# A post-norm decoder kernel: the end of its cross attention in one stage, top-k selection and first attention reordered

## The reference, cut to what matters

```
# block 2: cross attention
sim = einsum('bihd,bjhd->bhij', x @ Wq, ctx @ Wk) * SCALE
out = einsum('bhij,bjhd->bihd', softmax(sim), ctx @ Wv) @ Wo + bo
# block 5: 4 heads, 256 keys, the 32 greatest scores kept
scores = where(mask, Q K / sqrt(32), -inf)
topv, topi = top_k(scores, 32);  attn = scatter(softmax(topv), topi)
c_t = (mean of attn over the heads) @ V
x  = layernorm(x_text) * (1 + gate*scale_in) + gate*shift_in    # scale, shift = split(c_t @ W_film_in + b)
y  = s4d(x) * (1 + gate*scale_out) + gate*shift_out             # the same with W_film_out
xt = x_text + y
xt = xt + gelu(layernorm(xt) @ W1 + b1) @ W2 + b2
out5 = layernorm(xt) * g_norm_out + b_norm_out
x  = layernorm(x_text + out5)                                   # then block 6
```

## Time and profile before

| | |
|---|---|
| Median of 3 runs | 2426.15 us (2425.98 to 2428.31) |
| Profiled execution's own time | 2428.74 us |
| Its span, mean granted TensorE clock | 2426.9 us, 0.947 |
| PE busy | 2136.3 us (88%) |
| DVE busy | 1609.0 us (66%) |
| ACT busy | 999.0 us (41%) |
| POOL busy | 884.2 us (36%) |

### The profile page before, as it was taken

How to read it: one execution, slowest core, us unless ns; L and a number is a source line. 1 busy time by engine, 2 the same in 40 slices (tenths; PEclk the granted TensorE clock), 3 DMA queues, 4 the chain that set the end, 5 groups by cost and what they waited for, 6 DMA issues and landing times. The chain is left out here.

```text
span 2426.9 us, 33828 instructions
## 1 busy us (share of the span) xinstructions
PE 2136.3 (88%) x12230; PEld 1469.4 (61%) x12230; DVE 1609.0 (66%) x4155; ACT 999.0 (41%) x2097; POOL 884.2 (36%) x510
## 2 busy tenths in 40 slices
PE   8688888998997899499896888999698899999997
PEld 3255555642664789266474444447555788888886
DVE  6799999722657212456326999512489888888886
ACT  2498988511765331435424776141101321221210
POOL 0298888201541895324102655512301211101110
PEclk9799999999998999699998888999899999999998
DMA  3121111000005567300101000110210000000001
GB/s 100 47 81 48 49 48 49 9 11 0 1 1 177 193 204 240 113 1 2 59 1 42 1 1 1 42 78 1 89 51 3 1 1 1 1 1 1 1 1 36
DMA packets 63274, 108.56 MB, mean 45 GB/s; under 512 B 12482, under 2 KB 44098, under 8 KB 61444
## 3 DMA queue, kind: packets, MB, share of 16 engines
q1 hardware_dynamic: 61572, 102.20, 12.6%
q0 software_dynamic: 1536, 4.20, 0.5%
HBM read 93.40 MB, written 12.98 MB: 44 GB/s over the span
## 5 line engine op out<-in xcount | busy, mean ns | idle before, releaser
L766 POOL TENSOR_TENSOR XT<-mamba_DU,scan_BS 128x1024 f32<-128x1024 f32 x128 | 299.0, 2364 | 144.9 <-DMA scan_BS<-mamba_rows 107.5
L895 DVE TENSOR_TENSOR_SCAN scan_H<-scan_AB,XT 128x512 f32<-128x512 f32 x256 | 296.2, 1208 | 7.9 <-POOL XT L766 4.9
L3129 PE MATMUL ex_HP<-XT,pe_DOWN 128*128 128x256 f32 x1024 | 250.2, 391 | 6.0 <-PEq L2865 5.2
L3190 ACT ACTIVATE ex_GH<-ex_HP 128x512 f32<-128x512 f32 x128 | 76.4, 598 | 381.0 <-PE ex_HP L3129 346.2
L3160 PE MATMUL ex_OP<-pe_UP,ex_GH 128*128 128x256 f32 x1024 | 231.5, 380 | 0.0
L780 PEld LDWEIGHTS scan_TP<-ident,scan_H 128*128 128x128 f32 x1024 | 120.2, 142 | 156.9 <-DVE scan_H L895 81.1
L825 ACT ACTIVATE scan_AB<-mamba_E,mamba_AA 128x510 f32<-128x510 f32 x256 | 198.6, 776 | 37.6 <-DVE scan_H L895 33.2
L3129 PEld LDWEIGHTS ex_HP<-XT,pe_DOWN 128*128 128x128 f32 x1024 | 194.6, 195 | 31.6 <-issue 5.3
L3160 PEld LDWEIGHTS ex_OP<-pe_UP,ex_GH 128*128 128x128 f32 x1024 | 194.5, 191 | 25.8
L789 PE MATMUL scan_YT<-mamba_BC,ident 128*128 128x512 f32 x384 | 198.4, 599 | 4.1 <-ACT scan_YS L841 2.3
L780 PE MATMUL scan_TP<-ident,scan_H 128*128 128x128 f32 x1024 | 147.7, 278 | 45.6 <-DVE scan_H L895 45.5
(11 more groups left out here) (449 smaller groups left out, 4434.0 us busy)
## 6 DMA issues: line engine op xcount, KB each, us to landing
moe_W<-in_L_ffn_w SPq DMA_DIRECT2D x32, 1024.0 KB, 7.6
scan_BS<-mamba_rows SPq DMA_DIRECT2D x64, 256.0 KB, 3.2
pe_DOWN<-in_L_ffn_down SPq DMA_DIRECT2D x1, 4096.0 KB, 13.2
pe_UP<-in_L_ffn_up SPq DMA_DIRECT2D x1, 4096.0 KB, 22.5
moe_dispatch<-moe_BOTH SPq DMA_DIRECT2D x1, 2560.0 KB, 14.6
experts_XE<-moe_dispatch SPq DMA_DIRECT2D x16, 160.0 KB, 2.4
moe_answers<-experts_YE SPq DMA_DIRECT2D x16, 160.0 KB, 3.3
XT<-in_xT SPq DMA_DIRECT2D x4, 512.0 KB, 5.7
```

Of the source, the lines that this page charges most:

```text
L766: pool.tensor_tensor(BU[:, r % 2, cs], tokens(DU, cs, r // DS), row, ALU.mult).then_inc(bu_ready, 1)
L895: v.tensor_tensor_scan(H[:, r % 2, c], AB[:, n % 2, :], BU[:, r % 2, c], 0.0, ALU.mult, ALU.add).then_inc(h_ready, 1)
L3129: ins = pe.matmul(HP[:, n % 2, a, :], DOWN[:, k, 2 * q + a, :], XT[:, k, b * BLK:(b + 1) * BLK], start=(k == 0), stop=(k == KD - 1))
```

## The change

First attention: the one addition of BO to X is gone; after each of the 32 products POOL adds one half of BO (128 columns) to one half of a tile of X. Top-k: NM is made by ACT, at the head of `exp_all`, and DVE's L2458 is gone; ACT and DVE wait on the last strike of round 0. ACT's sums stand ahead of the copy of the pooled context, and the out half of film is a step of its own, between them. On PE the out half of unit n-2 is made between turn and pooled context of unit n-1, the in half at the end as before. At the start scores 0 come after the first queries, scores 1 after the third, and the square root, reciprocal and offset of the input norm are taken later on ACT and DVE. The end of block 5: `finish_norm` and `norm_gram` are replaced by one stage `finish_gram`, tile by tile, with 2 PSUM banks for residuals and 2 for transposes.

```diff
+                HALVES = NU // NT
                 out_loads.wait(pool)
-                add_row(pool, X, BO)
                 for m in range(NU):
                     pool.wait_ge(sum_ready, m + 1)
                     if m >= 2:
                         pool.wait_ge(turned, 2 * (m - 1))
                     pool.tensor_tensor(PN[:, m % 2], PR[:, m % 2], SM[:, m, :].rearrange("p (j o) -> p j o", o=1).to_broadcast([P, 4, S]),
                                        ALU.mult).then_inc(probs_ready, 1)
+                    part = slice(m % HALVES * (D // HALVES), (m % HALVES + 1) * (D // HALVES))
+                    pool.tensor_tensor(X[:, m // HALVES, part], X[:, m // HALVES, part], BO[:, part], ALU.add)
...
-            finish_norm(nc, "s4ln3", X, None, ident, mlp_product(HT, W2), total=lambda t: Z[:, t, :],
-                        base=lambda t: Z[:, t, :], out=lambda t: Z[:, t, :], affine=GB, needs=[mlp_loads])
-        norm_gram(nc, "s4norm", X, Z, XT, ident, FO, next_inputs.GS)
+            finish_gram(nc, "s4end", X, Z, XT, ident, FO, next_inputs.GS, mlp_product(HT, W2), GB, mlp_loads)
...
-                def film(n):
-                    for i in range(2):
-                        if n:
-                            pe.wait_ge(film_out_read if i else film_in_read, n)
+                    else:
+                        pe.wait_ge(film_out_read if i else film_in_read, n)
...
+                        pe.matmul(FP[:, i, :], CTT[:, k, n * P:(n + 1) * P], WI[:, i, k, :], start=(k == 0), stop=False)
+                    add_bias(pe, ident, FP[:, i, :], BI[:, i, :]).then_inc(film_ready, 1)
                 inputs.loads.wait(pe)
                 queries(0)
+                scores(0)
                 queries(1)
-                scores(0)
                 queries(2)
+                scores(1)
                 queries(3)
-                scores(1)
                 film_loads.wait(pe)
                 for n in range(NT + 1):
                     if n + 2 < NT:
                         scores(n + 2)
+                    if n == NT:
+                        film(n - 2, 1)
                     if n:
                         turn(n - 1)
+                    if 2 <= n < NT:
+                        film(n - 2, 1)
+                    if n:
                         pool_context(n - 1)
-                        film(n - 1)
+                        film(n - 1, 0)
+                film(NT - 1, 1)
...
                 def exp_all(n):
-                    act.wait_ge(max_ready, n + 1)
+                    act.wait_ge(first_struck, n + 1)
+                    act.activation(NM[:, n % 2, :], MX[:, n % 2, :, 0], ACT.Copy, scale=-1.0).then_inc(shift_ready, 1)
+                    act.wait_ge(shift_ready, n + 1)
...
+                def film_out(n):
                     act.wait_ge(film_ready, 2 * n + 2)
                     act.activation(FO[:, n, :], FP[:, 1, :], ACT.Copy, scale=GATE[:]).then_inc(film_out_read, 1)
...
                 queries(0)
+                scale(0)
                 queries(1)
-                scale(0)
-                queries(2)
-                queries(3)
                 act.wait_ge(stats_ready, 1)
                 act.activation(RS[:], MV[:, :, 1], ACT.Sqrt, bias=ident[:, EPS5:EPS5 + 1]).then_inc(std_ready, 1)
+                queries(2)
                 scale(1)
+                queries(3)
                 film_loads.wait(act)
...
                     if n + 2 < NT:
                         scale(n + 2)
+                    if n < NT:
+                        sums(n)
+                    if n >= 2:
+                        film_out(n - 2)
                     if 1 <= n <= NT:
                         pooled_out(n - 1)
-                    if n < NT:
...
+                def norm_scale():
                     v.wait_ge(stats_ready, 1)
...
-                            if r:
+                            if r == 1 and i:
+                                v.wait_ge(first_struck, n + 1)
+                            elif r:
                                 ch.need(struck[i])
...
+                        if r == 1 and n == 0:
+                            norm_scale()
...
                             if r == LAST and i:
                                 ins.then_inc(struck_ready, 1)
+                            elif r == 0 and i:
+                                ins.then_inc(first_struck, 1)
                             else:
                                 struck[i] = ch.mark(ins)
-                        if r == 0:
-                            v.tensor_scalar(NM[:, n % 2, :], mx[:, :, 0], -1.0, None, ALU.mult).then_inc(max_ready, 1)
...
-def norm_gram(nc, name, X, base, XT, ident, XC, GS):
...
+def finish_gram(nc, name, X, Z, XT, ident, XC, GS, residual, affine, needs):
+    LATE = 4
...
             @block.tensor
             def _(pe):
                 def turn(t):
+                    pe.wait_ge(normed2, t + 1)
+                    if t >= 2:
+                        pe.wait_ge(turned_read, t - 1)
                     for k in range(KD):
+                        ins = pe.transpose(TP[:, t % 2, k * P:(k + 1) * P], X[:, t, k * P:(k + 1) * P], ident[:, 0:P])
                     ins.then_inc(turned, 1)
                     if t == 0:
                         pe.matmul(RP[:, 0:D], ident[:, ONES:ONES + P], X[:, 0, :], start=True, stop=True)
                         for k in range(KD):
                             ins = pe.matmul(RC[:, k:k + 1], X[:, 0, k * P:(k + 1) * P], ident[:, ONES:ONES + 1], start=True, stop=True)
                         ins.then_inc(row_ready, 1)
+                def gram(t):
+                    if t == 0:
+                        pe.wait_ge(ones_ready, 1)
+                    pe.wait_ge(centered, t + 1)
+                    for m in range(KD):
+                        ins = pe.matmul(GP[:, m, 0:GW_], XC[:, t, m * P:(m + 1) * P], XC[:, t, 0:GW_], start=(t == 0), stop=(t == NT - 1))
+                    return ins
+                needs.wait(pe)
+                for t in range(NT + LATE + 1):
+                    if t < NT:
+                        if t >= 2:
+                            pe.wait_ge(residual_read, t - 1)
+                        residual(pe, t, R[:, t % 2, 0:D]).then_inc(residual_ready, 1)
+                    if 0 <= t - LATE < NT:
+                        turn(t - LATE)
+                    if t > LATE:
+                        ins = gram(t - LATE - 1)
                 ins.then_inc(gram_ready, 1)
+            @block.vector
+            def _(v):
+                ch = Chain(v, dve_chain)
+                def total(t):
+                    v.wait_ge(residual_ready, t + 1)
+                    v.tensor_tensor(Z[:, t, :], R[:, t % 2, 0:D], Z[:, t, :], ALU.add).then_inc(residual_read, 1)
+                    v.wait_ge(residual_read, t + 1)
+                    ch.link(v.bn_stats(raw[:, 0, t % 2, :], Z[:, t, :]))
+                    v.bn_aggr(MV[:, 0, t, :], raw[:, 0, t % 2, :]).then_inc(stats_ready, 1)
+                def norm(t):
+                    v.wait_ge(stats_ready, t + 1)
+                    v.wait_ge(std_ready, t + 1)
+                    ch.link(v.reciprocal(RS[:, 0, t:t + 1], RS[:, 0, t:t + 1]))
+                    v.tensor_scalar(Z[:, t, :], Z[:, t, :], MV[:, 0, t, 0:1], RS[:, 0, t:t + 1], ALU.subtract, ALU.mult).then_inc(normed, 1)
+                def join(t):
+                    v.wait_ge(affine_done, t + 1)
+                    ch.link(v.tensor_tensor(X[:, t, :], X[:, t, :], Z[:, t, :], ALU.add))
+                    ch.link(v.bn_stats(raw[:, 1, t % 2, :], X[:, t, :]))
+                    v.bn_aggr(MV[:, 1, t, :], raw[:, 1, t % 2, :]).then_inc(stats2_ready, 1)
+                def norm2(t):
+                    v.wait_ge(stats2_ready, t + 1)
+                    v.wait_ge(std2_ready, t + 1)
+                    ch.link(v.reciprocal(RS[:, 1, t:t + 1], RS[:, 1, t:t + 1]))
+                    v.tensor_scalar(X[:, t, :], X[:, t, :], MV[:, 1, t, 0:1], RS[:, 1, t:t + 1], ALU.subtract, ALU.mult).then_inc(normed2, 1)
+                for t in range(NT + 2):
+                    if t < NT:
+                        total(t)
+                    if 0 <= t - 2 < NT:
+                        norm2(t - 2)
+                    if t < NT:
+                        norm(t)
+                    if 0 <= t - 1 < NT:
+                        join(t - 1)
+            @block.gpsimd
+            def _(pool):
+                ch = Chain(pool, pool_chain)
+                needs.wait(pool)
+                pool.memset(XC[:, :, D:GW_], 1.0).then_inc(ones_ready, 1)
+                for t in range(NT + 4):
+                    if t < NT:
+                        pool.wait_ge(normed, t + 1)
+                        ch.link(pool.tensor_tensor(Z[:, t, :], Z[:, t, :], affine[:, 0, :], ALU.mult))
+                        pool.tensor_tensor(Z[:, t, :], Z[:, t, :], affine[:, 1, :], ALU.add).then_inc(affine_done, 1)
+                    u = t - 4
+                    if u >= 0:
```

(78 more changed lines are left out.)

50 lines of the change are left out of this document (6 added, 44 removed).

## The result

The changed kernel takes 2398.16 us (median of 20 executions, 2391.08 to 2422.78) against 2426.51 (20, 2421.11 to 2451.26). The ratio is 0.9888, 95% interval 0.9857 to 0.9918, so it is faster: by 28 us between the medians, by 27 us by the ratio. The profiled execution's span is 2392.5 us against 2426.9. The executions of both kernels fall into two groups some 23 us apart (before 15 of 20 up to 2433 and 5 from 2446 on, after 13 up to 2399 and 7 from 2414 on), and both medians lie in the lower group. The 34.4 us between the two profiled spans are not all the change's.

The account below looks back on a forecast made before the run. Bounds: DVE kept out by POOL in attention's opening, DVE in top-k, PE in the first stage at block 5's end. Terms -6.5 - 15.4 - 2.3 + 2.5 - 10.2 = -31.9 us, from 2426.15 to 2394; range 2386 to 2406.

Parts of the forecast that it names:

- attention: First attention's opening: DVE's negation, kept out by POOL's big addition, falls from 6.40 to 0.35 us; -6.5 us in all.
- top-k units: Settled top-k units: DVE loses the negation, 1.03 us in each of 15 units, 12.83 to 11.80 us; -15.4 us net.
- top-k entry: Start of top-k: root no longer behind four queries (1.37 us), scores 0 ahead of second queries (0.9 us); -2.3 us.
- top-k tail: End of top-k: unit 14's late film halves stand ahead of the last turn; +2.5 us, bounds 0 and 3.5.
- end of block 5: One merged stage, tiles at 4.75 us, next stage starting at 1735.6 instead of 1745.80; -10.2 us.
- D: Rival, first attention: POOL's additions of BO delay its products, costing 14.4 us, total 2408.7; chance 0.03.
- the norm's reciprocal and offset now stand in that unit: First top-k unit: two short DVE instructions at 0.35 us add 0 to 0.7 us, net +0.1.
- My own sign of being wrong: Units above 12 us, PE idling over 1 us per end-stage tile, or attention's POOL products late by the addition before them.
- A: Rival, top-k: with the pooled copy late, PE or ACT holds units at 12.83 us; 15.4 less gain, 2409.7; chance 0.09.
- C: Rival, top-k: PE at its lower clock level, units 18 us, 84 us more in the stage, total 2493; chance 0.03.
- B: Rival, end stage: DVE-POOL locks stretch tiles to at most 6.0 us, 2408 (0.07); the other way 4.58 us, 2391.
- gram until 10.1: End of block 5: gram finishes 10.1 us after the last residual's addition, then 2.4 us to the next stage.

Follow-up runs that it names:

- the changed kernel's second profile: The changed kernel measured once more with nothing altered: median 2407.73 us, ratio 0.9899 to the kernel before.
- The filled kernel: Changed kernel plus ten unread products on PE (the long filling) in its wait behind the last residual: end stage 81.79 us, 1.80 less.
- the four moves: Changed kernel with early norm offset, text-mask factor on ScalarE, end-stage lag of three tiles, five filling products: median 2397.15 us, ratio 0.9846.
- The two kernels with lag of three and filling: Changed kernel with four combined moves, and the same with top-k's old order but negation and factor on ScalarE: medians 2397.15 and 2416.97 us.
- the one with the lag alone: Changed kernel with turn, centring and gram one tile earlier in the end stage (three tiles, not four): end stage 82.71 us, 0.9 less.

## Why the prediction was right, point by point

| term | predicted | profile | 
|---|---|---|
| attention | -6.5 | -6.2 |
| top-k units | -15.4 | -12.5 |
| top-k entry | -2.3 | -1.6 |
| top-k tail | +2.5 | +2.4 |
| end of block 5 | -10.2 | -9.0 |

- **Attention.** Right in mechanism and size. PE's upper level after the wait, the 0.5 in it, did not come: 2.08 us for the first products. D did not happen: POOL is idle for 0.52 us or more before every product.
- **Units.** The step 12.83 - 1.03 = 11.80 is exact. The mis-sized term is "the norm's reciprocal and offset now stand in that unit: between 0 and 0.7 us". With them the unit grew by 1.57 us (11.79 to 13.36) where +0.1 net was forecast, because the offset (1.63 us) is itself the kind of instruction that POOL keeps out, and I had priced it by its free duration. And "I see no new collision" was thought through for the attention only: the factor met the mask in two units, 0.92 + 0.37 us. With 1.47 for the first unit that is 2.8 of the 2.9 us. My own sign of being wrong, units above 12 us, came in three of the fifteen lengths. Rivals A and C did not happen. A had its condition: the pooled copy ends 0.72 us into the next unit in most units (0.75 forecast) and up to 4.1 in others, but within the units DVE is never idle for more than 0.04 us.
- **Entry and tail.** The first maxima were to come 10.87 - 2.3 = 8.6 us after the stage's start, and came at 9.29, in the changed kernel's second profile at 8.37; the old order's also vary, by 1.4. The tail came out as worked: the turn starts 6.08 us after exponentials that themselves start 0.5 us later behind the last maxima, 6.6 in all. That is in this execution; in the second profile the tail is 5.7 us longer than before's, not 2.4.
- **End.** Tiles of 4.62 us, between 4.58 and my 4.75: DVE's join issues 0.17 us ahead of POOL's scale (1693.97, 1694.14) and goes first, POOL's instruction takes 0.84 instead of 0.72. PE is busy throughout, so B in neither form decides. From the first residual to the last addition are 68.6 us, 69.8 forecast. The failed step is "gram until 10.1": I took gram at the earlier trace rows's 0.91 us a tile, but it runs at PE's lower level behind a wait. From DVE's last addition to the next stage are 14.97 us, not 12.6, though POOL's last centring is done after 8.1 us, where 9.0 was forecast. The filled kernel shows it.
- **The price of the whole.** The medians differ by 28.4 us where 32 were forecast; the three stages gave 5.0 less than forecast, and 2.1 in the convolution were not forecast at all. So the whole is short by about what the parts are short. That it is no worse is partly luck. 7 of the 20 executions of the changed kernel and 5 of those before are in the upper group, 23 us up, which no term of the sum knew of, and top-k itself is not one number: against a profile with the old order's later entry (233.5 us of top-k, in three of the four profiles of the old top-k) the part gives 14.6, nearly what I forecast, and the changed kernel's second profile takes 3.2 us more for top-k and convolution than its first.

What the Trainium skill (SBUF — State Buffer, Who interferes with whom) says of a VectorE instruction with two SBUF inputs beside GpSimd, that whoever issues first has the shared ports for its whole instruction while the other is blocked, agrees with the offset's 1.63 and the factor's 1.06 us, and its sentence that PE and ACT never wait for anyone with ScalarE's 0.20 and 0.47 beside POOL's big addition. The first was cited in the prediction for the end stage, and not carried to the instruction that the change moved.

## What to carry to other kernels

List which DVE instructions of a bound unit can be kept out (here tensor_scalar and scalar_tensor_tensor, even on 4 columns), and take them off, before reordering anything: the negation and the factor on ScalarE gave 1.03 and 0.22 us a unit, the reordering nothing in sum. When an instruction is moved, ask what POOL does at its new place. Price PE's work behind a wait by rows behind a wait, and judge parts of 0.3% by stage lengths with the untouched stages beside them.

## What the hardware showed that I had not expected

- Beside POOL's instruction, reciprocal (0.17, 0.18 us) and max8 (1.39 for four) keep their length, and ScalarE too.
- The same code's top-k with convolution took 343.7 us in three executions and 346.9 and 347.4 in two.
- What the shorter end stage gained did not reach the kernel's end. With the four moves PE was granted 0.85 in the next stage's first 40 us, in the changed kernel 1.00:

```profile
1727.80:1767.80 40.00, 34.03 (x138) 21.72 (x138) 24.23 (x187) 4.19 (x11) 3.32 (x11) 0.85 0.51 211
```

```profile
1711.40:1751.40 40.00, 33.36 (x158) 21.68 (x158) 28.89 (x224) 4.79 (x12) 3.73 (x12) 1.00 0.51 211
```

The two kernels with lag of three and filling had 0.85, the one with the lag alone 0.88, the one with the long filling 0.96, as the kernel before. Whether this follows from the shorter end, or is chance, one profile of each does not settle.
